# A decoder layer on one core: the mixer's output product moved one slot up, its residual and normalization likewise, GpSimd's sums and the load of x moved to other places in their queues

## The reference, cut to what matters

```
resid = x
...                                   # conv, silu, scan, gate -> y
y = y @ W_out.T + b_out
return y + resid
...
x = _layernorm(x + _L0_attn_ref(x, ...))
x = _layernorm(x + _L0_xattn_ref(x, ctx_1024, ctx_1024, ...))
x = _layernorm(x + _L0_ffn_ref(x, ...))
```

## Time and profile before

| | |
|---|---|
| three runs | 936.7, 935.19, 936.65 us; median 936.65 |
| the profiled execution | 935.7 us, of which the span 933.9 us |
| granted TensorE clock, mean | 0.937 |
| PE, PEld busy | 791.7 us (85%), 632.4 us (68%) |
| DVE, ACT, POOL busy | 581.5 us (62%), 402.1 us (43%), 356.0 us (38%) |
| `attend` | from about 144 us to about 620 us of the span |

### The profile page before, as it was taken

One profiled execution on the slowest core, in us unless ns is written; L12 is line 12 of the kernel. 1 busy time (PEld: TensorE's weight loads), 2 busy tenths in 40 slices (PEclk: granted clock), 3 DMA queues, 4 the chain that ended last, 5 costly groups with the idle time before them and its releaser, 6 DMA issues. The chain is left out here.

```text
span 933.9 us, 16891 instructions
## 1 busy us (share of the span) xinstructions
PE 791.7 (85%) x5933; PEld 632.4 (68%) x5933; DVE 581.5 (62%) x1410; ACT 402.1 (43%) x639; POOL 356.0 (38%) x290
## 2 busy tenths in 40 slices
PE   5999883589999999999999897872799999999992
PEld 3777662456666766666676664541699999999982
DVE  4888855465777777777777876532345554654542
ACT  4666540235545655555555555530433323422320
POOL 0333334433355545544545452232225134424422
PEclk9999887889999999999999999865799999999997
DMA  3115701554445434544554334003422243234000
GB/s 126 46 28 156 208 1 51 153 152 124 127 143 165 151 113 134 153 139 135 160 154 137 119 119 126 23 31 111 147 91 86 86 129 119 63 111 139 21 28 19
DMA packets 75913, 100.91 MB, mean 108 GB/s; under 512 B 10961, under 2 KB 63354, under 8 KB 75856
## 3 DMA queue, kind: packets, MB, share of 16 engines
q1 hardware_dynamic: 72400, 92.03, 33.1%
q0 software_dynamic: 3456, 8.13, 2.5%
HBM read 65.47 MB, written 35.74 MB: 108 GB/s over the span
## 5 line engine op out<-in xcount | busy, mean ns | idle before, releaser
L984 DVE TENSOR_REDUCE nmax<-ps_m 128x4 f32<-128x1024 f32 x128 | 156.6, 1223 | 52.5 <-PE ps_m L744 40.5
L938 ACT ACTIVATE pt<-ps_a 128x1024 f32<-128x1024 f32 x128 | 131.4, 1026 | 99.4 <-PE ps_a L754 75.8
L1249 ACT ACTIVATE hid<-ps_h 128x640 fp32r<-128x640 f32 x64 | 45.1, 705 | 151.0 <-PE ps_h L1189 151.0
L1189 PE MATMUL ps_h<-xt,w_hi 128*128 128x320 f32 x512 | 99.9, 317 | 1.0 <-DVE xt L1264 1.0
L1298 DVE SCALAR_TENSOR_TENSOR hid<-ps_h,hid 128x640 fp32r<-128x640 f32 x64 | 52.8, 824 | 56.0 <-ACT hid L1249 55.5
L744 PE MATMUL ps_m<-kst,qst 48*128 48x256 f32 x512 | 65.6, 334 | 25.6 <-DVE nmax L984 23.0
L1201 PE MATMUL ps_y<-w_hi,hid 128*128 128x256 f32 x640 | 85.3, 284 | 1.7 <-issue 1.7
L1189 PEld LDWEIGHTS ps_h<-xt,w_hi 128*128 128x128 f32 x512 | 79.9, 191 | 5.5 <-DVE hid L1298 3.0
L1201 PEld LDWEIGHTS ps_y<-w_hi,hid 128*128 128x128 f32 x640 | 80.1, 191 | 1.9 <-issue 1.9
L744 PEld LDWEIGHTS ps_m<-kst,qst 48*128 48x128 f32 x512 | 39.1, 188 | 61.3 <-DVE nmax L984 32.3
L621 POOL TENSOR_TENSOR half<-kq,half 128x512 fp32r<-128x512 f32 x32 | 41.6, 1301 | 96.6 <-ACT half L876 91.7
(11 more groups left out here) (169 smaller groups left out, 1586.9 us busy)
## 6 DMA issues: line engine op xcount, KB each, us to landing
halves_dram<-half SPq DMA_DIRECT2D x64, 256.0 KB, 2.5
gated<-in_w SPq DMA_DIRECT2D x16, 1024.0 KB, 5.4
kst<-halves_dram SPq DMA_DIRECT2D x64, 128.0 KB, 2.6
qst<-halves_dram SPq DMA_DIRECT2D x64, 128.0 KB, 3.0
rows_dram<-blank SPq DMA_DIRECT2D x1, 5160.0 KB, 19.6
gated<-rows_dram SPq DMA_DIRECT2D x8, 645.0 KB, 4.2
x_raw<-in_x_t SPq DMA_DIRECT2D x8, 512.0 KB, 3.9
xres<-in_x SPq DMA_DIRECT2D x16, 256.0 KB, 3.4
```

What stands on the lines that cost most here:

```text
L938: nc.scalar.activation(pt[:, k % 4].rearrange("p s t q -> p (s t q)"), ps_a[:].rearrange("p s t q -> p (s t q)"), ACT.Exp).then_inc(s["exp ...
L984: nc.vector.tensor_reduce(nmax[:, q, :, :, h // 2].rearrange("p t s -> p s t"), ps_m[:], AX.X, ALU.max, negate=True).then_inc(s["max_done" ...
L1189: mm = pe.matmul(ps_h[:, f % 2, c2, 0:HC], w1[a][:, p, k, f * P:(f + 1) * P], xt[:, b, p, k, c2 * HC:(c2 + 1) * HC], start=(n == 0 and k = ...
L1249: nc.scalar.activation(hid[:, HI, f, :].rearrange("p (c n) -> p c n", c=2), ps_h[:, f % 2, :, 0:HC], ACT.Relu).then_inc(s["hid_hi"], 1)
```

## The change

TensorE issues the halves of `mixer_out` in slots 10 and 12. VectorE does `r1`, its statistics and `ve1` in slot 12, behind that slot's maximum, and `x1` in slot 13, ahead of the last maximum. GpSimd does `residual(n+1)` at the start of the step, from step 4 on behind `x2_done` (the payload, L991). SyncE loads x of n+2 behind the first half of the queries, in place of x of n+1 near the step's start.

```diff
@@ SyncE, load_x
             def step(n, p):
                 if on(n, -2):
                     load_s(n + 2, p)
-                if on(n, 0) and on(n, -1):
-                    load_x(n + 1, 1 - p)
...
                 if on(n, 0):
                     queries_in(n, p, 0)
+                if on(n, -1) and on(n, -2):
+                    load_x(n + 2, p)
@@ GpSimd
                 q = 1 - p
+                if on(n, 0) and on(n, -1):
+                    if on(n, 4):
+                        pool.wait_ge(s["x2_done"], n - 3)
+                    residual(n + 1, q)
                 if on(n, 0):
                     split_lo(n, s["k_hi"], s["k_split"])
...
-                if on(n, 0) and on(n, -1):
-                    residual(n + 1, q)
@@ TensorE
-                    if h in (11, 13) and on(n, -1):
-                        mixer_out(n + 1, (h - 11) // 2)
+                    if h in (10, 12) and on(n, -1):
+                        mixer_out(n + 1, (h - 10) // 2)
@@ VectorE
-                    if h == 13 and on(n, -1):
+                    if h == 12 and on(n, -1):
                         dve.wait_ge(s["wout_mm"], n + 2)
                         dve.wait_ge(s["x_added"], n + 2)
...
-                    if h == 13 and on(n, -1):
+                    if h == 12 and on(n, -1):
                         mean_var(dc, st1, mv1, s["stats1"], n + 1)
...
-                    if h == 14 and on(n, -1):
+                    if h == 13 and on(n, -1):
                         dve.wait_ge(s["rstd1"], n + 2)
```

## The result

The changed kernel takes **955.12 us** (median of 4 runs, 954.72 to 955.36), the kernel before 936.67 us on the same chip (4 runs, 935.19 to 938.51). The ratio is 1.019, with a 95% interval of 1.0172 to 1.0208. Slower was forecast, but by 8.3 us; it is 18.45 us, and the time lies above the range.

A forecast was written before the change was run, and what follows sets the result against it. TensorE, busy 24.8 of a steady step's 26.6 us, was taken as the bound. Steady steps 1.2, steps 1 to 3 3.75, step 0 2.5 and clock 1.7 us sum to 9.15 on 935.7: 944.9, given as 945.0 us; range 940.5 to 951.5.

The forecast's parts named there:

- TensorE's part, cost and gain 0: Slots 10 to 13: TensorE's instruction list stays the same, so the product ends no earlier; cost and gain 0.
- `r1` gains 0.77 us in steady steps: VectorE's `r1` no longer waits for GpSimd's second sum and starts 0.77 us earlier in each of 11 steps.
- The root's way, 0.91 us behind `r1`: `x1` idles 0.83 us for the root via GpSimd, and 0.08 us of overlap is lost: `r2` 0.91 us later.
- Step 0, +2.5 us: GpSimd's two sums stand ahead of `k_split(0)`, so the keys of step 1 start 2.5 us later.
- Steps 1 to 3, +3.75 us: GpSimd was not late here, so VectorE's order costs +1.26, +1.58 and +0.91 us at starts of steps 2 to 4.
- GpSimd's sums beside other work ... Cost 0: Steps 4 to 14: `k_split` 0.4 us later, `ve3` held 0.4 us under idle time; cost 0, up to 8 us.
- The clock, +1.7 us, bounds 0 and 3.4: One more fall of TensorE's clock, at the longer idle heads of steps 2 and 3: +1.7 us.
- rival 2: VectorE is held by GpSimd's sums, 0.3 to 0.75 us a step: 948 to 953 us; chance 0.10.
- Rival 1: TensorE's clock falls in many steady steps at the 1.47 us head gap: 950 to 964 us; chance 0.12.
- Rivals 3 to 5: 3: opening hidden, 938 to 941, 0.08; 4: root's way short, 931.6, 0.03; 5: no change, 935 to 938.5, 0.04.

The follow-up runs named there:

- e3: Kernel before with only the product's slots on TensorE changed from 11 and 13 to 10 and 12: 936.89 us, ratio 0.9987.
- e5: Kernel before with only GpSimd's sums moved, from behind the scatters to between `q_split` and the scatters: 930.57 us, ratio 0.9895.
- e8: Kernel before with GpSimd's sums moved between the wait for the payload and the scatters: 928.27 us, ratio 0.9893.
- e4: Changed kernel with GpSimd's sums moved from the step's start to behind `q_split`, ahead of the scatters: 949.86 us, ratio 1.0103.
- e2: Kernel before with only VectorE's order changed (`r1` to `ve1` in slot 12, `x1` in slot 13): 960.2 us, ratio 1.0224.
- e6: Changed kernel with filler matmuls on TensorE in the opening (12 and 18 in step 0, 8 and 10 at heads of steps 2 and 3): 950.31 us.
- e11: Kernel before with filler matmuls on TensorE, 22 at slot 15 of step 0 and 4 at the head of step 3: 937.34 us, ratio 0.999.
- e10: Changed kernel with `q_split` waiting for `y` in steps 4 to 14, sums still at the step's start: 951.09 us, ratio 1.0143.
- e1: Kernel before with only GpSimd's sums and SyncE's load of x at their new places: 935.84 us, ratio 0.9972.
- e9: Kernel before with GpSimd's sums between the payload wait and the scatters, plus 22 and 4 filler matmuls on TensorE in steps 0 and 3: 924.99 us, ratio 0.9869.

## Why the prediction was right and where it failed

It had the direction and the price of VectorE's order right, and missed two terms of its sum: what GpSimd's sums cost beside other work, and the clock. Of the signs that it gave for being wrong one came: `ve3` and its neighbours are long in each of steps 6 to 13. Of those for being right one failed: a steady step lasts 27.48 and 27.96 us, not 26.6 to 27.0. Taken by its own steps:

- **TensorE's part, cost and gain 0**: right. e3 shows it, with 0.9987 and an interval that holds 1.
- **`r1` gains 0.77 us in steady steps**: right. e5 and e8, where the sums are early and VectorE's order is the old one, win 0.45 and 0.75 us a step; in e5 `carry` takes the difference.
- **The root's way, 0.91 us behind `r1`**: right, shown three times: 0.93 in the timeline after, 0.90 and 0.91 between e4 and e5, 0.93 between e2 and before. The two rows of steps -1 and 0 had priced it.
- **Step 0, +2.5 us**: right. The keys of step 1 start 180.27 - 151.3 = 29.0 us behind the first `y`, and started 177.88 - 151.5 = 26.4 us behind it: +2.6. e4, with the sums out of that place, has 26.1. Not in the forecast was that TensorE stands 3.29 us in front of the product of step 0, where it stood 1.02 us, while its wait for the context is shorter (4.71 in place of 6.19 us).
- **Steps 1 to 3, +3.75 us**: about right. The heads of steps 2 and 3 idle 2.54 and 2.93 us (1.85 and 2.89 forecast), that of step 4 1.46 us. With step 0 the forecast for the waits was 6.25 us; the comparison of e6 and e11 gives 5.5 to 6.7.
- **Steady steps, "GpSimd's sums beside other work ... Cost 0": the step that failed.** It is a mis-sized term of the sum: not 0, but 0.77 us in each of steps 6 to 13, some 6 us; the steady part grew by 7.6 us where +1.2 was forecast. The mechanism stood there, with its upper bound of 0.75 us a step, and as rival 2 with 0.10. I had found one held operation (`ve3`, 0.4 us) and laid it against 0.52 us of idle time behind it. That much was right: `ve3` lost 0.49 us and the idle time took it up. The runs show what it left out: the sums push `k_split`, the root and `twice` back as well (`k_split` by 0.4 us was even in the text), `expert` and `slot0` take longer beside the later `twice`, 0.24 + 0.21 = 0.45 us with no idle time behind, and by this `y` has moved far enough for its last operation to begin behind `q_split`, 1.05 us more, of which 0.30 reach the step. e10 shows the two parts, and e4, e5 and e8 that all of it comes from where the sums stand. Put by edits, moving the sums is worth nothing in a steady step (e1: 0.77 us won at `r1`, as much lost ahead of it), and the root's way costs its 0.91 us.
- **The clock, +1.7 us, bounds 0 and 3.4: the second term that failed.** It is 6.4 to 7.6 us in the profiled pair, all in the opening, and 3 to 4 us against e3's execution, so its size is known only roughly. I priced one fall at a head by a steady step. But the opening has several gaps close together (3.29, 4.71, 2.54 and 2.93 us on TensorE), and step 1 between them ran at the low level for 15 of its 28 us (clock 0.73, before 0.92). That the clock is a cause and not a companion is shown by e6: filled gaps, clock at 0.95, and 4.8 us less for all its overlength.

The sum is then 1.2 + 6.2 in the steady part, 13.1 in the opening (waits and clock together) and 1 less behind step 15: 19.5 us, the difference of the spans. The timed medians differ by 18.45 us; beside the later medians of before, 937.49 to 938.78 us, it is 16.3 to 17.6.

**The rivals.** Rival 2 happened, and in full: 8.3 + 6.2 us would have been 951, inside its 948 to 953. Rival 1, falls in many steady steps, did not happen in the changed kernel (one in eleven, as before), but did in e2. Its 964 for falls in all eleven read more out of the Trainium skill ("TensorE: Matmul & The Clock Gate", HAM oscillation) than stands there: the kernel described there waits 3 to 5 us for a transfer at each tile, and the gap here is 1.48 us. Rivals 3 to 5 did not: nothing of the opening was hidden, and `x1` idled 0.84 us each time, not below 0.3. The Trainium skill ("Advanced Engine Details and Errata", GPSIMD Details) names two kinds of VectorE's instructions as in conflict with GpSimd: those in a two-port mode and those with two SBUF inputs. `y` at 2.72 in place of 1.67 us and `carry` at 1.25 in place of 0.15 us agree with the second. `ve3`, `expert` and `slot0` have one input each; only the first could cover them, and no run here shows in which mode they ran. It would not tell either why `expert` is long beside `twice` here and not before.

**What stays open.** Why `expert` and `slot0` are held in the changed kernel, e1 and e10, but not before, where `twice` ran beside them too (393.04 to 395.50, `expert` at 393.78 with 0.17 us). What length of filler holds the clock. How much of the clock's share is the sums' delay in step 0 and how much the later heads: e4 has the first gap as before and only the heads longer, and its opening lasts 107.8 us at 0.84, but e8, with neither, has 104.6 us at 0.82 and e3 102.5 at 0.85, so the spread between executions hides it; no version changes the heads alone at a held clock. And no version moves the load of x alone: it is in e1, e4 and the changed kernel, and the 0.91 us between e4 and e5, like the 0.93 of e2 without it, leaves it nothing in a steady step.

## What to carry to other kernels

When a piece of GpSimd's work is moved, follow everything behind it in its queue, and lay each shifted piece beside VectorE's operations, those with two SBUF operands first: one meeting can be covered, but each delay moves VectorE on into the next one. Price a result that goes from VectorE to GpSimd and back by its whole round trip (0.84 us of VectorE's idle time here for a 128x2 operation) unless something useful stands in between; the old order had the maximum there. And price new idle time near other idle time of TensorE with the clock at its low level for the work in between, not for one gap: here that was 3 to 7.6 us, where the waits of the opening cost about 6.

The best version found is e9: the order of the kernel before, GpSimd's sums behind the wait for the payload's places, and filler in the opening, at 0.9869 of the time before. The move of the sums alone (e8) has 0.9893, so the filler's share is small and uncertain.

## What was not expected of the hardware

- A tiny operation of VectorE can be held for nearly the whole of a GpSimd operation: `carry`, 128x8 bf16, took 1.25 us beside a sum of 1.26 us, and 0.15 us elsewhere. `ve3`, 128x2, took 0.66, ending 0.03 us behind the sum beside it.
- Which of two meeting operations is held turned on 0.03 us: the last of the four operations of `y` took 1.53 us when it began 0.03 us behind a GpSimd operation of 1.28 us. Where it had begun first, `y` kept its 1.67 us, and GpSimd's took 1.36 us in place of 1.27.
- The clock of the same program differs from execution to execution in the opening: a mean of 0.90 and 0.85 in before and e3, with openings of 98.7 and 102.5 us. In one hour the kernel before ran between 935.06 and 942.8 us (17 runs), so that a comparison at 0.2% needs many runs.
- Gaps of about 1.48 us once in a step left the clock at its full level in ten of eleven steps; gaps of 2.1 to 2.5 us lost it in about half.
